# Local attention scores of two head pairs in two row halves of TensorE, and a prefetch hint on TensorE's loops

## The reference

```python
def local_attention(q, k, v):          # 16 heads of 64, windows of 32 tokens
    ...
    bk2, bv2 = (look(bk), look(bv))    # each window and the one before it
    ...
    sim = jnp.einsum('bhwie,bhwje->bhwij', bq, bk2) * QK_SCALE
    sim = jnp.where(mask, -jnp.finfo(sim.dtype).max, sim)
    attn = jax.nn.softmax(sim, -1)
    out = jnp.einsum('bhwij,bhwje->bhwie', attn, bv2)
...
for i in range(DEPTH):                 # DEPTH = 6
    x = attn_layer(shift_tokens(x), Wqkv[i], q_scale[i], k_scale[i], Wo[i]) + x
    x = ffn_layer(shift_tokens(x), ln_g[i], ln_b[i], W1[i], b1[i], W2[i], b2[i]) + x
```

## Time and profile before

| | |
|---|---|
| time, median of 3 runs | 5555.22 us (5555.07 to 5568.53) |
| the profiled execution | 5561.1 us, of which the span is 5559.3 us |
| TensorE busy | 4882.0 us (88%) |
| VectorE busy | 3969.7 us (71%) |
| local stack (from about 680 to 4640 us) | 48 passes; a pass in the loops takes about 82 us |
| mean granted TensorE clock | 0.947 of 2.4 GHz |

### The profile page before, as it was taken

How to read it: one execution, slowest core, us unless ns; L and a number is a source line. 1 busy time by engine, 2 the same in 40 slices (tenths; PEclk the granted TensorE clock), 3 DMA queues, 4 the chain that set the end, 5 groups by cost and what they waited for, 6 DMA issues and landing times. The chain is left out here.

```text
span 5559.3 us, 91306 instructions
## 1 busy us (share of the span) xinstructions
PE 4882.0 (88%) x33904; PEld 2705.3 (49%) x34096; DVE 3969.7 (71%) x5868; ACT 2274.5 (41%) x3178; POOL 2001.0 (36%) x1547
## 2 busy tenths in 40 slices
PE   5999689999999999999899999999999996577786
PEld 2222255555555555555555555555555554222222
DVE  4677378778778777877777877877777774466663
ACT  0666434334333433333333433433343342045554
POOL 1111044444444444444444444444444442211110
PEclk7999889999999999999999999999999998588898
DMA  2222112122222122112212222212222221122210
GB/s 56 55 47 47 50 48 51 48 52 64 54 51 53 49 63 61 48 48 52 69 49 52 52 60 59 52 46 52 52 56 51 53 49 49 30 47 47 46 25 17
DMA packets 181030, 279.66 MB, mean 50 GB/s; under 512 B 58032, under 2 KB 79792, under 8 KB 174896
## 3 DMA queue, kind: packets, MB, share of 16 engines
q1 hardware_dynamic: 180880, 277.66, 20.6%
HBM read 61.70 MB, written 17.56 MB: 14 GB/s over the span
## 5 line engine op out<-in xcount | busy, mean ns | idle before, releaser
L792 POOL TENSOR_TENSOR l_u<-l_t 128x512 f32<-128x512 f32 x384 | 486.6, 1267 | 1904.8 <-DVE l_t L894 1904.8
L894 DVE SCALAR_TENSOR_TENSOR l_t<-l_r,l_qkvec,l_tab 128x1024 f32<-128x1024 f32 x768 | 941.5, 1267 | 29.5 <-ACT l_sq L822 25.1
L470 DVE TENSOR_REDUCE a_nmax<-a_pair 128x2 f32<-128x1024 f32 x512 | 612.5, 1221 | 385.1 <-PE a_pair L550 383.0
L1079 PE MATMUL l_r<-l_kbd,l_qn 128*32 128x256 f32 x12288 | 771.4, 389 | 67.4 <-DMA l_kbd<-l_kn 48.2
L388 ACT ACTIVATE a_pt<-a_st 128x512 f32<-128x512 f32 x1024 | 579.8, 597 | 342.7 <-PE a_st L534 332.5
L1079 PEld LDWEIGHTS l_r<-l_kbd,l_qn 128*32 128x32 f32 x12288 | 421.6, 110 | 280.2 <-issue 130.1
L1117 PE MATMUL l_r<-l_pbd,l_va 128*64 128x160 f32 (+1 forms) x6144 | 442.7, 296 | 125.0 <-DMA l_pbd<-l_pt 125.0
L534 PE MATMUL a_st<-a_qs,a_ks 75*128 75x512 bf16 x1024 | 394.4, 400 | 149.7 <-ACT a_pt L388 75.2
L801 POOL TENSOR_TENSOR l_p<-l_p,l_srec 128x1024 f32<-128x1024 f32 x192 | 365.5, 1904 | 378.0 <-DVE l_srec L963 251.7
L844 ACT ACTIVATE l_p<-l_p 128x1024 f32<-128x1024 f32 x192 | 203.2, 1058 | 718.7 <-DVE l_p L945 718.7
L1117 PEld LDWEIGHTS l_r<-l_pbd,l_va 128*64 128x64 f32 x6144 | 399.9, 137 | 191.2 <-issue 191.2
(11 more groups left out here) (183 smaller groups left out, 7207.3 us busy)
## 6 DMA issues: line engine op xcount, KB each, us to landing
l_kbd<-l_kn SPq DMA_DIRECT2D x1536, 64.0 KB, 2.0
l_pbd<-l_pt SPq DMA_DIRECT2D x1344, 64.0 KB, 2.0
a_ks<-a_scr SPq DMA_DIRECT2D x96, 192.0 KB
a_qs<-a_scr SPq DMA_DIRECT2D x288, 64.0 KB
a_scr<-a_parts SPq DMA_DIRECT2D x48, 256.0 KB, 2.5
l_wqkv<-in_wqkv SPq DMA_DIRECT2D x6, 1536.0 KB, 6.8
l_pbd<-l_pt SPq DMA_DIRECT2D x192, 48.0 KB, 1.9
l_wo<-in_wo SPq DMA_DIRECT2D x6, 512.0 KB, 3.9
```

Of the source, the lines that this page charges most:

```text
L470: nc.vector.tensor_reduce(out=nmax[:, n, 2 * i:2 * i + 2], in_=pair[i][:], op=ALU.max, axis=AX.X, negate=True).then_inc(pair_dve[i], 1)
L792: nc.gpsimd.tensor_tensor(u[buf][:, 2 * a, :], t[:, 0, :], t[:, 3, :], ALU.subtract)
L894: last = nc.vector.scalar_tensor_tensor(out=t[:, 2 * half:2 * half + 2, :], in0=R[a][:, half, :].unsqueeze(1).to_broadcast([D, 2, T]), sca ...
L1079: last = nc.tensor.matmul(R[3][q:q + 32, bank, 256 * (w // 4):256 * (w // 4) + 256], qn[:, half, WIN * W:WIN * W + WIN], kbd[half][:, :, W ...
```

## The change

It has two parts.

The **scores**: a key block `kbd` has two head slots per feature instead of four, since two heads (one pair) take 64 of the 128 rows. Each product now has 64 rows (one pair of heads) and streams 128 columns instead of 128 rows and 256 columns. The pairs alternate in the code: pair 0 lies in rows 0 to 63 and writes bank 0 of `R[3]`, pair 1 in rows 64 to 127 and writes bank 1. There are 64 products in a step instead of 32. Both mask products come first. With them the order of the softmax units changes (pair, window group, side of the pair instead of window group, head), and so do the mask, the offset into `pbd` in line 1117 (in the new code 1123), and the last of the `pbd` DMAs, which copies 448 instead of 384 columns. VectorE, ScalarE and GpSimd run the same instructions on the same shapes.

The **hint**: `layers` builds its loops with `hint_back_edge=True` on TensorE. Other engines keep theirs without.

```diff
-        kbd = [sb(f"kbd{i}", [D, CH, KC]) for i in range(2)]
+        kbd = [sb(f"kbd{i}", [D, 2, KC]) for i in range(2)]
...
-        def layers(eng, body):
+        def layers(eng, body, hinted=False):
+
+            def loop(first, end):
+                return nc.Fori(first, end, engines=[eng.engine], hint_back_edge=hinted)
...
-                with eng.Fori(1, NB) as b:
+                with loop(1, NB) as b:
...
-                        sp.dma_start(band[96:128, NT, 0:(NT - 1) * CH * WIN],
-                                     turned[0:32, 0, CH:, :].rearrange("p u i -> p (u i)")).then_inc(pbd_full[c % 2], 16)
+                        sp.dma_start(band[96:128, NT, 0:(NT * CH - 2) * WIN],
+                                     turned[0:32, 0, 2:, :].rearrange("p u i -> p (u i)")).then_inc(pbd_full[c % 2], 16)
...
-                                sp.dma_start(kbd[i][q, r, WIN:KC], kn[q, i, :]).then_inc(S["kbd_full"], 16)
+                                sp.dma_start(kbd[i][q, r % 2, WIN:KC], kn[q, i, :]).then_inc(S["kbd_full"], 16)
...
-                            for w in range(8):
-                                W, q = 8 * bank + w, 32 * (w % 4)
-                                for half in range(2):
-                                    last = nc.tensor.matmul(R[3][q:q + 32, bank, 256 * (w // 4):256 * (w // 4) + 256],
-                                                            qn[:, half, WIN * W:WIN * W + WIN], kbd[half][:, :, WIN * W:WIN * W + 2 * WIN],
-                                                            start=False, stop=(half == 1), skip_group_check=True)
+                        for g in range(NT):
+                            for half in range(2):
+                                for w in range(4):
+                                    for pair in range(2):
+                                        W, heads = 4 * g + w, slice(64 * pair, 64 * pair + 64)
+                                        last = nc.tensor.matmul(R[3][32 * w:32 * w + 32, pair, 128 * g:128 * g + 128],
+                                                                qn[heads, half, WIN * W:WIN * W + WIN],
+                                                                kbd[half][heads, :, WIN * W:WIN * W + 2 * WIN],
+                                                                start=False, stop=(half == 1), skip_group_check=True)
...
-                                    o = (g * CH + h) * WIN
+                                    o = ((bank * NT + g) * 2 + side) * WIN
...
-            layers(pe, body)
+            layers(pe, body, hinted=True)
```

More of the change, by code:

```diff
@@ L707, in local_stack @@
         block = ctx.enter_context(nc.Block())
-        def layers(eng, body):
+        def layers(eng, body, hinted=False):
+            def loop(first, end):
+                return nc.Fori(first, end, engines=[eng.engine], hint_back_edge=hinted)
             def layer(par, l, last=False):
                 body(par, l, "last layer" if last else "layer", 0, NB - 1)
-                with eng.Fori(1, NB) as b:
+                with loop(1, NB) as b:
                     body(par, l, None, b, b - 1)
             body(0, 0, "layer", 0, None)
-            with eng.Fori(1, NB) as b:
+            with loop(1, NB) as b:
                 body(0, 0, None, b, b - 1)
-            with eng.Fori(0, DEPTH // 2 - 1) as i:
+            with loop(0, DEPTH // 2 - 1) as i:
                 layer(1, 2 * i + 1)
@@ L1395, in layouts @@
     first = hidden | ((np.arange(D)[:, None] < WIN) & (j < WIN))
-    tiles = [first] + [hidden] * (NT - 1)
-    a["mask"] = np.concatenate([np.tile(m, (1, CH)) for m in tiles], axis=1).astype(np.float32) * np.float32(MASKED)
+    tiles = ([first] + [hidden] * (NT - 1)) * 2
+    a["mask"] = np.concatenate([np.tile(m, (1, 2)) for m in tiles], axis=1).astype(np.float32) * np.float32(MASKED)
     a["d_wr"], a["d_wk"], a["d_wv"] = (g[f"L1_ffn_W_{n}"].T for n in "rkv")
```

## The result

The changed kernel took **5588.07 us** (median of 11 runs, 5564.17 to 5601.18); the kernel before, run beside it, 5555.07. The ratio is 1.0059, with a 95% interval of 1.0035 to 1.0083: 33 us slower, where the prediction had 14 us faster. The profiled execution took 5580.92 us, of which the span is 5579.1 (5561.1 and 5559.3 before).

A forecast was written before the change was run, and what follows sets the result against it. VectorE's and the DMA's cycles bound steps 0, 1, 3, scores only step 2. With 11 us kept of 57 and 3 from the outer edge, 5561.1 - 11 - 3 = 5547; from the median 5541 us, range 5493 to 5600.

The forecast's parts named there:

- What bounds the kernel: Per step of a pass: VectorE's and the DMA's cycles set steps 0, 1, 3; scores lie on the path only in step 2.
- The score block: Step 2, first mask product to transposes: 4.44 us falls to 2.5 to 3.0, its 128 sweeps taking 1.9 to 2.4.
- the burst of the earlier trace: Nearest quick row of TensorE's trace: four sweeps started within 0.05 us, so 128 would take 1.6 us.
- the bulk row: Slowest TensorE row: 32 sweeps in 1.90 us, 59 ns a sweep; as issue pace it would make 7.6 us.
- The gain of step 2: Transposes wait for ScalarE's `rnx`, so step 2 gains 1.2 us, not 2; over 47 passes 57 us.
- The clock: TensorE drops to 1.2 GHz in new stops before line 1117, steps 0 and 1; only 11 us of the gain stays.
- the locking of passes at 81.9: A pass of 80.75 us shifts the stretch until it meets a new stop; then 81.95, with the stretch at the same place.
- slower, by the clock alone: Rival: low stretches in steps 0 and 1 of one pass, 2.4 us lost against 1.2 gained; 5611 at most; chance 0.10.
- The code: Rival: TensorE's longer loop no longer stays resident, back edges stop 2.97 us each; 5605, up to 5660; chance 0.15.
- the hint's cover: Clause of the code rival: back edges stop unless the hint fetches ahead; if it covers, seven fetches a pass remain.
- The hint itself: TensorE's loop back edges: saves up to 3 us on the outer edge; cost 0 to 0.2 us times 36 edges, taken as 0.
- The range: Whole kernel's time: from the full gain, 5493, to 5600 us, leaving out the larger half of the two slower cases.

The follow-up runs named there:

- the version that keeps the clock: Changed kernel plus unread products in steps 0 and 1, three ahead of the transposes and seven ahead of line 1123: 5493.09 us, 0.989 of the kernel before.

## Why the prediction was wrong, point by point

**What bounds the kernel: right.** Steps 0, 1 and 3 keep their length whatever the scores take. The stops that I expected there, 2.05 us ahead of line 1117 and up to 0.7 ahead of the transposes, are 1.94 and 0.93, and a pass saves only what step 2 saves.

**The score block: right.** About 2.6 us with both mask products, where I took 2.5 to 3.0, and 2.03 of it for the sweeps, where I took 1.9 to 2.4. 128 sweeps in 2.03 us are 16 ns each, close to the burst of the earlier trace rows that I had chosen over the bulk row. The page of the Trainium skill that allows no starts closer than 25 ns (TensorE: Matmul & The Clock Gate, "Wait — 56ns, not 53.3ns?") does not hold over these 128 sweeps. The run with the halves one after the other agrees with it, 3.31 / 128 is 26 ns, but agrees as well with columns: 0.107 us for a sweep, as the prediction worked it out, four at a time, is 27 ns. These runs do not tell the two apart.

**The gain of step 2: right.** 1.2 us a pass, bounded by ScalarE's `rnx`: 81.97 less 80.74 is 1.23. The threshold held too: it gave the whole gain to any block under 3.2 us, and with the halves one after the other (3.55 us and 0.2 for the mask product without a record) a pass lost 0.53 of it. In the version that keeps the clock, the 45 passes save 3707.0 - 3655.9 = 51 us; by the prediction's price, 45 x 1.2 = 54.

**The clock: the step that failed.** It named the mechanism, the place (steps 0 and 1, ahead of line 1117), the price of one stretch there (1.2 us; the ones at 29.4 us cost 1.15) and even the locking of passes at 81.9. It was mis-sized in three ways.
- The stretch in step 0 is mostly twice as long (17 of 25), 6.8 us, and covers the whole of line 1123 and a part of line 1028: 4.32 + 2.75 for 2.29 + 2.27 is 2.5 us. A pass with it takes 83.1 us, 2.35 more. The four of the earlier trace rows are of the single length, and I took that for the length. Single ones in both steps of a pass, as my rival had it, came too, with the same 83.1 us.
- I let a pass that loses 1.2 us wait there, at 81.95, for good. Passes change place instead: rows of 81.9 end in one of 84.3, and passes of 80.74 and 83.1 alternate, mean 81.9, which gains nothing over before either.
- The first two passes of a layer, in which more DMA traffic runs (a DMA share of 0.25 in the one shown, against 0.21), got stretches in both steps in nine of ten cases: 83.6 to 88.2 us, where they had been 82.0 to 84.7. These ten passes alone make 25 of the 40 us lost. I had expected a pass or two of each layer to gain 1.2 us.

In the sum: 38 of 45 passes with a stretch in steps 0 to 2. The clock's price is 3746.6 - 3655.9 = 91 us, or 2.4 a pass of those; less the 51 us gained, 40 us are lost, which is the difference of the two sums. I had put it at 46 us (57 gained, 11 kept). This is the rival "slower, by the clock alone", with my price of 2.4 us a pass. I had given it 0.10, because seven of eight stops of 1.78 us or more in the trace of before had left the clock alone. The weight was laid wrongly. Seven of those eight stood in steps 0 and 1, all in the first two passes of a layer, six of them in pairs in one pass, and none of the seven had a pause ahead of its transposes; the change puts one into both steps of every pass, with a pause of 0.6 to 0.9 us ahead of it. What the trace of before could tell was that such stops sometimes do it, one in eight; after the change it was 52 of 88. What raised that share, the pause, the shorter scores before it or the place in the pass, no run separates, and a chance of a half would have been honest.

**The code: right on the danger, and the hint's cover was the cause of its not coming.** The price of an edge, 2.97 us, was 2.6 to 3.2 on 26 edges without the hint. The price of the whole was mis-sized: 5660 us at most, where 5807 were measured (1.047), because the clock is low behind each such stop too. That the hint covers it had been a clause of that rival; it deserved a sentence of its own, since it means that the two parts of the change can't be had apart.

**The hint itself: wrong.** I took its cost as 0, out of bounds of 0 to 7 us, and a gain of 3 us on the outer edge. The edge was not helped (2.96 in the changed kernel, 3.26 with the hint alone) and a hand-over stop of 3.44 us came up: 0.28% in all, 17 us of which 10 are not located. In the changed kernel this matters little: with the filling its passes and those of the kernel without hint and with half of the products differ by 7 us.

**The range** held the time; the direction it did not.

## What to carry to other kernels

Work taken off an engine that waits elsewhere becomes longer stops, and on TensorE a stop is not free: look where the clock falls already, how long TensorE stops there, and count how many stops of that length the change will make. That most of the few such stops before did no harm says little. If the gain is swallowed so, fill the longest stop with products that nobody reads, sized a little under the wait (seven 512-column bf16 products for 1.9 us here), and leave alone those stops behind which nothing is late. Size the products for the kernel at hand: the same ones in the kernel before, whose stops were shorter, cost 1%. A loop that has grown by half a thousand instructions may live by its hint alone; the loop that fitted paid 0.28% for one.

## What the runs showed of the hardware that I had not expected

- In the passes of the changed kernel a stretch at 1.2 GHz was of 3.4 us or of twice that, 6.8; before the change 17 of 18 were of the single length, after it 17 of 25 in step 0 were double.
- Two row halves of TensorE, given small products in turn, take 16 ns a sweep (2.03 us for 128); the same products ordered by half, 26 ns (3.31 us).
- Filling 1.5 of 1.9 us in two of four steps brought low time in steps 0 to 2 from 249 us to 7 or less; a pause of 0.7 to 0.9 us and one of 0.4 us were left in each of the two steps.
- A loop of some 1710 TensorE instructions is fetched anew in most passes without the hint (343 blocks, stops on 25 of 36 inner back edges, none of them in the first layer's loop) and stays with it (116 blocks, no such stop).
